# State-space stage of a two-layer transformer kernel: magnitudes by quarter, the end of exp(x)-1 on VectorE, small inputs and head-weight loads at other places of the order

## The reference, cut to what matters

```
dt  = exp(log_dt)                                    # 32
A   = -exp(log_A_real) + 1j * A_imag                 # 32 x 64
dtA = A * dt[:, None]
Ct  = C * (exp(dtA) - 1) / A                         # the coefficients
K   = 2 * einsum('hn,hnl->hl', Ct, exp(dtA[:, :, None] * arange(512))).real
y   = causal_convolution(u, K) + u * D[:, None]      # per position h, over 512 lags
y   = y * (arange(512) < length[:, None])            # mask
```

## Time and profile before

| | us |
|---|---|
| median of 3 runs | 2147.5 (2145.01 to 2147.85) |
| the profiled execution, its own time | 2145.5 |
| its span, first to last instruction | 2143.7 |
| TensorE busy, x11876 matmuls | 2100.7 (98% of the span) |
| VectorE busy | 1389.0 (65%) |
| GpSimd busy | 1249.7 (58%) |
| ScalarE busy | 724.1 (34%) |
| VectorE busy from 0 to 20, 20 to 40, 40 to 60, 60 to 80 us | 13.69, 14.50, 18.54, 16.24 |
| TensorE busy in the same | 10.75, 16.15, 19.80, 16.48 |

### The profile page before, as it was taken

The page is one execution under the profiler, slowest core; times in us unless marked ns, Lnnn a source line. Parts: engine busy times, 40 slices in busy tenths (PEclk is TensorE's granted clock), DMA queues, the critical chain, the costliest instruction groups (busy, mean ns, idle before and its releaser), DMA issues. The chain is left out here.

```text
span 2143.7 us, 36830 instructions
## 1 busy us (share of the span) xinstructions
PE 2100.7 (98%) x11876; PEld 1816.5 (85%) x11876; DVE 1389.0 (65%) x2620; ACT 724.1 (34%) x1447; POOL 1249.7 (58%) x1315
## 2 busy tenths in 40 slices
PE   7899999999999999999999999999999999999999
PEld 5788888989898898989888898988887777878887
DVE  7767777676767767665656656565666676654444
ACT  5333232332223232332323233232333644443332
POOL 3587585777757676776757676675844732114220
PEclk9999999999999999999999999999999999999999
DMA  7421213111111226211111111111112200001110
GB/s 239 152 57 50 53 44 86 54 48 50 49 51 44 72 59 220 56 40 40 40 39 53 55 49 39 39 39 39 41 60 83 94 9 0 0 0 40 39 39 20
DMA packets 122613, 122.26 MB, mean 57 GB/s; under 512 B 35249, under 2 KB 101457, under 8 KB 120497
## 3 DMA queue, kind: packets, MB, share of 16 engines
q1 hardware_dynamic: 91697, 109.87, 16.5%
q10 hardware_dynamic: 29568, 7.34, 1.6%
q0 software_dynamic: 1280, 4.20, 0.7%
HBM read 108.13 MB, written 13.28 MB: 57 GB/s over the span
## 5 line engine op out<-in xcount | busy, mean ns | idle before, releaser
L215 PE MATMUL psum<-yc,wh 128*128 128x512 f32 x904 | 362.0, 400 | 5.2 <-DVE yc L1488 4.6
L216 PE MATMUL psum<-yc,wh 128*128 128x512 f32 x904 | 353.5, 391 | 0.0
L217 PE MATMUL psum<-yc,wh 128*128 128x512 f32 x904 | 353.4, 391 | 0.0
L1370 DVE TENSOR_TENSOR resid<-psum,resid 128x512 f32<-128x512 f32 x248 | 171.1, 691 | 138.1 <-PE psum L217 133.8
L215 PE MATMUL psum<-kept,yc 128*128 128x256 f32 x896 | 256.6, 286 | 2.8 <-DVE u L1320 1.1
L217 PE MATMUL psum<-kept,yc 128*128 128x256 f32 x896 | 253.4, 283 | 0.0
L216 PE MATMUL psum<-kept,yc 128*128 128x256 f32 x896 | 253.4, 283 | 0.0
L941 POOL TENSOR_TENSOR wh<-wh_f,wh 128x256 fp32r<-128x256 f32 x256 | 189.4, 750 | 104.5 <-ACT wh L907 102.3
L941 POOL TENSOR_TENSOR wh<-raw,wh 128x256 fp32r<-128x256 f32 x192 | 142.0, 739 | 107.8 <-ACT wh L907 107.8
L215 PEld LDWEIGHTS psum<-yc,wh 128*128 128x128 f32 x904 | 170.8, 189 | 37.9 <-DVE yc L1488 5.4
L217 PEld LDWEIGHTS psum<-yc,wh 128*128 128x128 f32 x904 | 170.3, 188 | 36.3
(11 more groups left out here) (355 smaller groups left out, 4916.5 us busy)
## 6 DMA issues: line engine op xcount, KB each, us to landing
raw<-in_attn_w SPq DMA_DIRECT2D x96, 512.0 KB, 5.0
wo_f<-in_attn_w SPq DMA_DIRECT2D x31, 512.0 KB, 4.0
hankel<-kernel_rows SPq DMA_DIRECT2D x32, 256.0 KB, 4.9
y_parts<-stage ACTq DMA_DIRECT2D x56, 128.0 KB, 2.3
yc<-y_parts SPq DMA_DIRECT2D x7, 1024.0 KB, 5.0
resid<-in_xT SPq DMA_DIRECT2D x4, 1024.0 KB, 9.8
outT<-wide SPq DMA_DIRECT2D x16, 256.0 KB, 2.5
kept_f<-in_l_w SPq DMA_DIRECT2D x3, 1024.0 KB, 5.6
```

Of the source, the lines that this page charges most:

```text
L215: pe.matmul(out, w[0], x[0], start=start, stop=False)
L216: pe.matmul(out, w[0], x[1], start=False, stop=False)
L217: return pe.matmul(out, w[1], x[0], start=False, stop=stop)
L1370: dve.tensor_tensor(part, psum[:, 5 + (GH + m) % 3, :], part, ALU.add).then_inc(tail_free, 1)
```

## The change

The magnitudes are made in two parts, 8 positions (the first quarter) ahead of `coefficients()` and 24 behind `kernels(0)`, and ScalarE takes their exp in two parts, the second behind `by_channel(0)`. GpSimd computes exp(x)-1 up to the fourth of six polynomial terms and the subtraction of 1 from 2^k; the last two terms, the product and the sum are done by VectorE inside `coefficients()`. `small_inputs()` is split in two: its first six operations stand behind `tables(1)`, the other five (`small_tables()`) behind `mask_turn(0, 0)`. The two loads of head weights stand on SyncE behind the first quarter's Hankel loads, so that the four small loads follow those of x directly. The diff, whole:

```diff
--- before.py
+++ after.py
@@ -273,7 +273,10 @@
     return then, tt, ts, stt
 
 
-def exp_minus_1(then, tt, ts, stt, engine, x, em1, two_k, tmp):
+EXP_TERMS = (1 / 720.0, 1 / 120.0, 1 / 24.0, 1 / 6.0, 0.5, 1.0)
+
+
+def exp_minus_1(then, tt, ts, stt, engine, x, em1, two_k, tmp, terms=EXP_TERMS):
 
     t0, t1, t2 = tmp
     ts(t0, x, 1.4426950408889634, MAGIC, ALU.mult, ALU.add)
@@ -285,10 +288,19 @@
     then(engine.tensor_copy(two_k.bitcast(I32), t0))
     ts(t2, t1, 1 / 40320.0, 1 / 5040.0, ALU.mult, ALU.add)
     tt(t2, t2, t1, ALU.mult)
-    for c in (1 / 720.0, 1 / 120.0, 1 / 24.0, 1 / 6.0, 0.5, 1.0):
+    for c in terms:
+        stt(t2, t2, c, t1, ALU.add, ALU.mult)
+    ts(t0, two_k, 1.0, None, ALU.subtract)
+    if terms == EXP_TERMS:
+        exp_minus_1_end(tt, stt, em1, two_k, tmp, ())
+
+
+def exp_minus_1_end(tt, stt, em1, two_k, tmp, terms):
+
+    t0, t1, t2 = tmp
+    for c in terms:
         stt(t2, t2, c, t1, ALU.add, ALU.mult)
     tt(t2, t2, two_k, ALU.mult)
-    ts(t0, two_k, 1.0, None, ALU.subtract)
     tt(em1, t2, t0, ALU.add)
 
 
@@ -334,7 +346,7 @@
         dt, ar = prm[:, 0, :], prm[:, 1, :]
         ai, cr, ci = prm[:, 2, :], prm[:, 3, :], prm[:, 4, :]
         da, db, inv = sk[:, 5, 0:SEQ], sk[:, 6, 0:SEQ], sk[:, 18, 0:SEQ]
-        em1 = sk[:, 9, 0:SEQ]
+        em1, em1_tmp = sk[:, 9, 0:SEQ], [sk[:, i, 0:SEQ] for i in (11, 0, 1)]
         ctr, cti = sk[:, 19, 0:SEQ], sk[:, 20, 0:SEQ]
         lensi = sb(ctx, "lensi", [P, BATCH], I32)
         lens = sb(ctx, "lens", [P, BATCH])
@@ -422,8 +434,6 @@
             sp.dma_start(kernel_rows[:, DIM:RROW], t["zeros"]).then_inc(rows_stored, 16)
             for c in range(KC):
                 sp.dma_start(resid[:, c, :], t["xT"][c * P:(c + 1) * P, :]).then_inc(x_in, 16)
-            for k in range(2):
-                hw.load_head(sp, t, 0, 0, k)
             sp.dma_start(ffn[:, 0:4], t["c2_bias"]).then_inc(later_in, 16)
             sp.dma_start(l1[:, 0:32], t["l1_small"]).then_inc(later_in, 16)
             sp.dma_start(l1[:, 56:64], t["router_bias"]).then_inc(later_in, 16)
@@ -451,6 +461,8 @@
 
             store_rows(0)
             load_quarter(0)
+            for k in range(2):
+                hw.load_head(sp, t, 0, 0, k)
             for q in range(1, QUARTERS):
                 if q == QUARTERS - 1:
                     sp.wait_ge(comp_done, CROWS)
@@ -519,6 +531,12 @@
                 dve.wait_ge(trig_done, q + 2)
                 tt(right[:], theta[:, :, 2 * LI:], mag[:, part, LI:], ALU.mult)
 
+            def magnitudes(part):
+
+                n = part.stop - part.start
+                tt(mag[:, part, :], per_lag(da[:, part], LI + LJ), per_position(const("lags")[:, LI:], n), ALU.mult)
+                dve.sem_inc(mag_ready, 1)
+
             def coefficients():
 
                 s1, s2 = sk[:, 8, 0:SEQ], sk[:, 8, SEQ:]
@@ -532,6 +550,7 @@
 
                 stt(vers, s2, -2.0, s2, ALU.mult, ALU.mult)
                 dve.wait_ge(em1_ready, 1)
+                exp_minus_1_end(tt, stt, em1, sk[:, 10, 0:SEQ], em1_tmp, EXP_TERMS[4:])
                 stt(e1r, vers, 1.0, em1, ALU.add, ALU.mult)
                 tt(e1r, e1r, vers, ALU.add)
                 stt(e1i, em1, 1.0, s1, ALU.add, ALU.mult)
@@ -595,6 +614,8 @@
                 for k in range(2):
                     ts(later["label_mask"][:, k, :], ids[:, 0:BATCH], const("labeler")[:, k:k + 1], 0.5, ALU.is_equal, ALU.mult)
 
+            def small_tables():
+
                 rows_f = ids[:, BATCH:BATCH + BATCH // ABATCH]
                 ts(rows_f, rows_f, 0.0, ADA - 1.0, ALU.max, ALU.min)
                 ts(rows_f, rows_f, float(AR), const("adapter_rank"), ALU.mult, ALU.add)
@@ -608,8 +629,7 @@
             dve.sem_inc(bank_free, NCB)
             dve.wait_ge(const_in, 16)
             tables(0)
-            tt(mag[:], per_lag(da, LI + LJ), per_position(const("lags")[:, LI:], SEQ), ALU.mult)
-            dve.sem_inc(mag_ready, 1)
+            magnitudes(slice(0, NB))
             dve.wait_ge(trig_done, 1)
             coefficients()
             dve.wait_ge(mag_done, 1)
@@ -617,19 +637,22 @@
             left_factor(0)
             dve.wait_ge(params_in, 32)
             kernels(0)
+            magnitudes(slice(NB, SEQ))
             for q in range(1, QUARTERS):
                 tables(q)
                 if q == 1:
+                    small_inputs()
                     dve.wait_ge(mask_ready, KC)
+                    dve.wait_ge(mag_done, 2)
                 else:
                     mask_turn(q - 2, 2)
                     mask_turn(q - 2, 3)
                     differences(q - 2)
                 right_factor(q)
                 left_factor(q)
-                if q == 2:
-                    small_inputs()
                 mask_turn(q - 1, 0)
+                if q == 1:
+                    small_tables()
                 kernels(q)
                 mask_turn(q - 1, 1)
             mask_turn(QUARTERS - 2, 2)
@@ -699,9 +722,13 @@
             for k in range(1, KC + 1):
                 turned_weights(k)
             sines(0)
-            act.wait_ge(mag_ready, 1)
-            act.activation(mag[:], mag[:], ACT.Exp).then_inc(mag_done, 1)
+            def magnitudes(n, part):
+                act.wait_ge(mag_ready, n)
+                act.activation(mag[:, part, :], mag[:, part, :], ACT.Exp).then_inc(mag_done, 1)
+
+            magnitudes(1, slice(0, NB))
             by_channel(0)
+            magnitudes(2, slice(NB, SEQ))
             for i in range(3):
                 composite_wide(i)
             for i in range(3):
@@ -732,7 +759,7 @@
                 tt(out, spare, other, op1)
 
             pool.wait_ge(small_ready, 1)
-            exp_minus_1(then, tt, ts, stt, pool, da, em1, sk[:, 10, 0:SEQ], [sk[:, i, 0:SEQ] for i in (11, 12, 13)])
+            exp_minus_1(then, tt, ts, stt, pool, da, em1, sk[:, 10, 0:SEQ], em1_tmp, terms=EXP_TERMS[:4])
             pool.sem_inc(em1_ready, 1)
 
             pool.wait_ge(const_in, 16)
```

## The result

| | before | after |
|---|---|---|
| median of 20 runs each, us | 2146.88 (2143.55 to 2152.37) | 2142.15 (2139.64 to 2147.18) |
| ratio of after to before | | 0.9978, interval 0.9972 to 0.9985 |
| second set, 21 and 10 runs on another chip, us | 2146.38 | 2140.40 (2137.32 to 2144.30) |
| its ratio | | 0.9970, interval 0.9961 to 0.9980 |
| the profiled execution and its span | 2145.5, 2143.7 | 2141.0, 2139.2 |

The change makes the kernel 4.7 us faster (2146.88 - 2142.15; by the interval 3.2 to 6.0), where 5.2 us were forecast. The interval lies on both sides of 0.2%.

The account below looks back on a forecast made before the run. VectorE's list up to quarter 3's addition was taken to bound the state-space stage. 1.13 + 5.71 - 1.6 = 5.2 us, from 2146.5 to 2141.3 us; range 2137.5 to 2145.0.

Parts of the forecast that it names:

- The chain: State-space stage: quarter 3's Hankel load waits for the rows' store, this for VectorE's addition at 71.63, to come 5.2 us earlier.
- Quarter 0: Start of the stage: GpSimd's shorter exp(x)-1 brings the addition to 23.45 instead of 25.74; 1.2 us earlier if held 1.85 us.
- The cap: Quarter 0: TensorE ends composite(1) at 22.71, so its next step can start at most 2.28 us earlier.
- Quarter 1: Sine ready at 31.9, six small-input operations take 1.3 us, five 1.2 us; addition at 36.2, 1.13 us earlier.
- Contention: tables(3) on VectorE falls beside GpSimd's busy stretch and loses 1.6 us; bounds 0 and 2.7 us.
- the rival of full blocking: VectorE makes no headway while GpSimd works beside tables(3): gain 4.1 us, 2142.4 us; chance 13%.
- the sum: Whole stage: 1.13 (start and quarter 1) + 5.71 (small inputs off the path) - 1.6 (contention) = 5.2 us.
- Quarter 3: TensorE's convolution after quarter 2's Hankel matrices takes 5.0 us, not 6.66; kernels(3) at 65.5, addition at 66.4.
- the clock rival: New 1.2 us idle time before kernels(2) lowers TensorE's clock; up to 16 us by the stage's end, 2157; chance 5%.
- The first product: First matmul of attention on TensorE: at 86.0 instead of 91.25, with nothing changed between quarter 3's addition and it.
- The sign of being wrong: Addition of quarter 3 after 68, or at 66.4 without the start of attention following.
- The median: Whole kernel: 5.2 us subtracted from 2146.5, the mean of four executions, gives 2141.3 us.

Follow-up runs that it names:

- e3: The kernel after with the two head-weight loads back ahead of the four small loads on SyncE; ratio to before 0.9987.
- e6: The kernel after with seven transposes on TensorE in its wait before kernels(2); ratio to before 0.9973.
- e8: The kernel after with the edits of e7, six transposes behind the last convolution and ten ahead of attention's first product; ratio to before 0.9959.
- e9: The kernel after, unchanged, run again beside the kernel before on another chip; ratio to before 0.9970.
- e7: The kernel after with seven transposes before kernels(2), and GpSimd's low parts of quarter 0 made only with those of quarter 1; ratio to before 0.9974.
- e10: The kernel after with only six transposes behind the last convolution and ten ahead of attention's first product; ratio to before 0.9964.
- e5: The kernel after with the magnitudes in one piece ahead of coefficients() and one exp on ScalarE, as before; ratio to before 0.9969.
- e2: The kernel after with all eleven small-input operations back in quarter 2; ratio to before 0.9980.

## Why the prediction was right

- **The chain.** The addition of quarter 3 was the measure, and VectorE's list what bound it, but for quarter 3 in the first profile, where TensorE came last. Additions: 23.45 foretold and 23.42 measured; 36.2 and 36.40; 51.5 and 51.64.
- **Quarter 0.** GpSimd's last operation was 0.66 us and not 1.85, so VectorE didn't wait for it, and its first operation behind the magnitudes started at 17.01. The cap (TensorE's composite(1)) is real: where composite(0) ran at the low clock, in e3, e6, e8 and e9, the addition came at 24.9 to 25.5, and 1.5 to 2.1 of the 2.3 us were lost.
- **Quarter 1.** The sine was ready, the six operations took 1.4 us (1.3 foretold), the five 1.2 us (1.2).
- **Contention.** 1.6 us foretold, 1.77 measured (e7). Blocking was between the bounds: 1.22 us for an operation of 0.69, less than VectorE's and GpSimd's instruction one behind the other, so the rival of full blocking is out. GpSimd was slowed too, which the sum left out: its four operations took 3.9 us (53.02 to 56.89) and not 2.7. The sum came near since it goes by their number: 1.77 us is 0.44 for each, where 0.41 was taken.
- **Quarter 3, the step that was off.** I wrote that for the convolution "with no idle time before it I take 5.0". That one did take 4.92 us. What I had left out of the sum is the convolution behind the new idle time before kernels(2), which the clock rival names: it took 6.68 us, and TensorE was late by 1.7 us. The addition came at 67.72 instead of 66.4. Without that low stretch it comes at 66.81 (e10); 0.9 us was the clock's and 0.4 us VectorE's list. So the addition gained 3.9 us in the first profile and 4.8 in e10, where the sum has 5.2. The rival's mechanism came in one profile out of seven, for one stretch, and not for the rest of the stage. The prediction argued against it with the 1.57 us wait alone; the 2.28 us wait of the earlier trace rows, with no low clock behind it, was the stronger row.
- **The first product** came at 86.76 instead of 86.0. I held everything behind the addition to be fixed, and it isn't: it is 19.0 us to the first product after, 19.6 before and 20.0 in e10, mostly by how long the store of the rows took. In the first profile this gave 0.6 us back, and that is luck.
- **The sign of being wrong** was an addition of quarter 3 after 68. It came at 67.72, but in e9, the same kernel, at 68.32, since the low level at the start lasted longer. The sign was set closer than one execution differs from the next.
- **The parts.** I priced the head loads' move by a store that would wait; from e3's times that is some 0.7 us, an estimate, and the earlier Hankel matrices come on top. I didn't say that the split of the magnitudes is worth nothing, which e5 shows, though it followed from my own terms: 1.2 us won ahead of quarter 0's addition, 1.3 us paid behind.
- **The median.** 2141.3 foretold, 2142.15 and 2140.40 measured. At an equal mean clock the two sets leave about 4 us for the order of the work, by the estimate above; that they lie on both sides of the forecast is in part the clock's doing, and so luck.

## What to carry to other kernels

Find the one event from which on nothing changes, and reckon each edit by how much earlier that event comes; small operations are free in a wait (the eleven here took 5.7 us where most ran beside GpSimd, and 2.7 us where it was idle). A change of a few us in a stage is told by a profile only when it is known where the low clock fell in it: compare intervals between two events that have none, and more than one profile of the same kernel. The mean clock of each timed run is a help too. Work moved out of a wait on one engine may open a wait on another; ask what the clock does behind it.

## What the runs showed that I had not expected

- The granted clock's low stretches lie at another place in each execution of the same kernel: after had them at 52.1 and 86.2 us, e9 from 88.8 to 95.6 us, and at the start until 17.1. The wait of 1.0 to 1.7 us before kernels(2) was followed by one in one profile of seven, waits of 2.0 to 2.8 us in four cases of seven.
- The trace's clock entries start late, at 11.1 to 17.9 us: in e9 the products from 13.57 us on run at half pace while the window shows 1.00. Durations of equal products tell it.
- The step from the store of eight rows to the first load of them took 1.53 us in most cases and up to 3.51 (quarter 1 of e5).
- x (4 MB in four loads) landed at 24.58 in e2 and at 22.85 to 23.22 in before, after, e3 and e9, with the same loads ahead of it, and an issue on SyncE took 3.70 us once (e3) where it mostly takes 0.43.
